# A conditioned attention, SwiGLU and ternary-MLP kernel: the order of the first batch's start on each engine, and finer waits there

## What is computed

```python
gamma, beta = t @ attn_gamma_w.T, t @ attn_beta_w.T        # per batch, 256 each
h = gamma * rmsnorm(x) + beta
q, k, v = h @ W_q.T, h @ W_k.T, h @ W_v.T                   # 16 heads of 16
x = x + alpha * (softmax(scale * q k^T) v) @ W_o.T
x = x + f_alpha * swiglu(f_gamma * rmsnorm(x) + f_beta)     # 1024 hidden
h = x * (1 + cond @ norm_w.T) * rsqrt(mean(x*x) + eps)
val, gate = split(h @ up_w.T)                               # 2 x 1024
y = act_quant(val * gelu(gate)) @ weight_quant(down_w).T + x
```

## Time and profile before

| what | value |
|---|---|
| median of 3 runs | 1111.65 us |
| lowest and highest run | 1110.89 and 1113.03 us |
| the profiled execution, own time | 1110.89 us |
| its span in the profile | 1109.1 us |
| its mean granted TensorE clock | 0.98 |
| busy: PE, DVE, ACT, POOL | 1037.1, 774.6, 562.6, 347.4 us |

### The profile page before, as it was taken

How to read it: one execution, slowest core, us unless ns; L and a number is a source line. 1 busy time by engine, 2 the same in 40 slices (tenths; PEclk the granted TensorE clock), 3 DMA queues, 4 the chain that set the end, 5 groups by cost and what they waited for, 6 DMA issues and landing times.

```text
span 1109.1 us, 19198 instructions
## 1 busy us (share of the span) xinstructions
PE 1037.1 (94%) x6775; PEld 719.0 (65%) x6775; DVE 774.6 (70%) x1556; ACT 562.6 (51%) x1260; POOL 347.4 (31%) x415
## 2 busy tenths in 40 slices
PE   6789889999999999999999999988989999899997
PEld 5333247755774775577567567744878878788775
DVE  4766686677578757866876696677647787466775
ACT  4355666557556655755665575556552333132221
POOL 2501123323242332424133332201332444243331
PEclk9889999999999999999999999998999999999998
DMA  8554433064234406332531623060311210002111
GB/s 252 150 92 154 76 104 132 15 110 125 87 45 111 148 21 111 101 111 30 121 116 58 111 71 123 12 139 20 97 53 29 59 57 30 29 29 63 58 53 38
DMA packets 89375, 92.71 MB, mean 84 GB/s; under 512 B 11856, under 2 KB 86616, under 8 KB 88256
## 3 DMA queue, kind: packets, MB, share of 16 engines
q1 hardware_dynamic: 87248, 89.59, 31.1%
q10 hardware_dynamic: 2032, 1.90, 0.6%
HBM read 61.68 MB, written 29.78 MB: 82 GB/s over the span
## 4 chain that ended last, share of the span: by engine, by line
PE 77%; DVE 14%; issue 5%; DMA 2%; POOL 1%; ACT 1%; ACTq 0%; POOLq 0%; DVEq 0%
PE gen L1162 30%; PE core L1162 13%; PE pvb L1277 11%; PE core L1251 9%; PE core L1265 8%; DVE negmax L924 7%; PE gen L1488 2%; PE pvb L1480 1%; PE gen L1236 1%; DVE o L948 1%; PE pvb L1285 1%; PE gen L1315 1%; PE core L1255 1%; DVE qs L1112 1%; DMA shift_d<-shift 0%
## 5 line engine op out<-in xcount | busy, mean ns | idle before, releaser
L924 DVE TENSOR_REDUCE negmax<-core 128x1 f32<-128x512 f32 x512 | 337.5, 684 | 169.9 <-PE core L1251 169.0
L712 ACT ACTIVATE p<-core 128x512 f32<-128x512 f32 x512 | 278.5, 597 | 146.1 <-PE core L1265 143.5
L1162 PE MATMUL gen<-hs,wgh 128*128 128x256 f32 x1536 | 220.5, 294 | 9.7 <-DVE a L978 9.7
L1251 PE MATMUL core<-kst,qst 96*128 96x512 bf16 x512 | 193.7, 395 | 33.5 <-DVE negmax L924 27.7
L1162 PEld LDWEIGHTS gen<-hs,wgh 128*128 128x128 f32 x1536 | 196.2, 189 | 28.3 <-DVE a L978 14.8
L1162 PE MATMUL core<-wup,hp 128*128 128x512 f32 x768 | 190.7, 397 | 0.9 <-POOL hp L652 0.9
L603 POOL TENSOR_TENSOR a<-a 128x256 fp32r<-128x256 f32 x128 | 94.7, 740 | 290.3 <-ACT a L730 287.7
L1162 PEld LDWEIGHTS core<-wup,hp 128*128 128x128 f32 x768 | 140.2, 189 | 29.2 <-issue 0.9
L1265 PE MATMUL core<-qst,kst 99*128 99x512 bf16 x512 | 157.2, 387 | 0.1
L1251 PEld LDWEIGHTS core<-kst,qst 96*128 96x128 bf16 x512 | 46.0, 97 | 152.3 <-DVE negmax L924 77.4
L1277 PE MATMUL pvb<-p,vst 128*32 128x512 f32 x1024 | 127.7, 618 | 0.0
(11 more groups left out here) (158 smaller groups left out, 1234.0 us busy)
## 6 DMA issues: line engine op xcount, KB each, us to landing
parts_d<-qk SPq DMA_DIRECT2D x30, 384.0 KB, 2.7
v_d<-v SPq DMA_DIRECT2D x8, 1024.0 KB, 3.9
vst<-v_d SPq DMA_DIRECT2D x16, 512.0 KB, 5.4
qst<-parts_d SPq DMA_DIRECT2D x96, 64.0 KB, 2.3
qst<-parts_d SPq DMA_DIRECT2D x48, 128.0 KB, 4.5
kst<-parts_d SPq DMA_DIRECT2D x48, 128.0 KB, 7.7
kst<-parts_d SPq DMA_DIRECT2D x91, 64.0 KB, 2.3
xr<-in_x_dram SPq DMA_DIRECT2D x8, 512.0 KB, 4.0
```

The source lines that it names most:

```text
L712: act.activation(p32[:, ring(b, m), k * S:(k + 1) * S], stb[k], ACT.Exp, scale=SCALE).then_inc(s["exp_"], 1)
L924: dve.tensor_reduce(negmax[:, n // TT, n % TT:n % TT + 1], smb[n % 2], AX_X, ALU.max, negate=True).then_inc(s["smax"], 1)
L1162: last = pe.matmul(out_, l, r, start=start and i == 0, stop=stop and i == len(passes) - 1, **kw)
L1251: pe.matmul(smb[n % 2], qst[0:KROWS, h, q * P:(q + 1) * P], kst[0:KROWS, h, :], start=True, stop=True).then_inc(s["smax_mm"], 1)
```

## The change

Five edits, all of them in the start of batch 0:

1. DVE normalises x and splits weight group 0 before it waits for the tables' matmuls; the copies to `table` and `cur` follow (now `first_tables`).
2. The load of W_v has a semaphore of its own. Weight group 0 waits for W_q and W_k alone; groups 1 and 2 wait for W_v too.
3. The first projection waits for the low parts of two weight groups, the second for those of three.
4. The low part of K's first half is made by DVE behind `qk_rest(0, 1)` in place of POOL. It has a semaphore of its own (`first_kl`), for which SP, POOL and ACT wait where they waited for `qk_l`.
5. ACT issues the store of K's high part behind the middle part of Q and not ahead of it.

```diff
-                sp.wait_ge(s["qk_l"], 2)
+                sp.wait_ge(s["first_kl"], 1)
                 first_part(sp, 1, 2, "parts1_st")
...
-                pool.tensor_tensor(qk3[:, j % 2, 2, :], rest[j], qk3[:, j % 2, 1, :], ALU.subtract).then_inc(s["qk_l"], 1)
+                if (b, j) == (0, 2):
+                    pool.wait_ge(s["first_kl"], 1)
+                if (b, j) != (0, 1):
+                    pool.tensor_tensor(qk3[:, j % 2, 2, :], rest[j], qk3[:, j % 2, 1, :], ALU.subtract).then_inc(s["qk_l"], 2 if (b, j) == (0, 2) else 1)
...
-                act.dma_start(raw_qkv[...], w[n]...).then_inc(s["raw_qkv_load"], 16)
+                act.dma_start(raw_qkv[...], w[n]...).then_inc(s["raw_v_load" if n == "W_v" else "raw_qk_load"], 16)
...
                 act.copy(qk3[:, j % 2, 0, :], gen[QK_BANK[j]][:, :]).then_inc(s["qk_h"], 1)
-                if (b, j) == (0, 1):
-                    act.wait_ge(s["qk_h"], 2)
-                    first_part(act, 1, 0, "first_kh")
...
-                    act.wait_ge(s["qk_l"], j - 1)
+                    act.wait_ge(s[("qk_l", "first_kl")[j % 2]], 1)
                 act.copy(qk3[:, j % 2, 1, :], rest[j]).then_inc(s["qk_m"], 1)
+                if (b, j) == (0, 0):
+                    act.wait_ge(s["qk_h"], 2)
+                    first_part(act, 1, 0, "first_kh")
...
-            dve.wait_ge(s["tab_mm"], 1)
             nt, nf = NSC * KD, NFIRST * KD
-            dve.tensor_copy(table[:, 0:nf, :]..., gen[1][:, 0:nf * B]).then_inc(s["tab_copy"], 1)
+            def first_tables():
+                dve.wait_ge(s["tab_mm"], 1)
+                dve.tensor_copy(table[:, 0:nf, :]..., gen[1][:, 0:nf * B]).then_inc(s["tab_copy"], 1)
+                dve.wait_ge(s["tab_copy"], 1)
+                dve.tensor_copy(cur[:, 0, 0:nf].unsqueeze(2), table[:, 0:nf, bass.ds(0, 1)]).then_inc(s["cur_set"], 1)
...
                 dve.tensor_tensor(rest[j], gen[QK_BANK[j]][:, :], qk3[:, j % 2, 0, :], ALU.subtract).then_inc(s["qk_r"], 1)
+                if (b, j) == (0, 1):
+                    dve.wait_ge(s["qk_m"], 2)
+                    dve.tensor_tensor(qk3[:, 1, 2, :], rest[1], qk3[:, 1, 1, :], ALU.subtract).then_inc(s["first_kl"], 1)
...
                         if b == 0:
-                            dve.wait_ge(s["tab_copy"], 1)
-                            dve.tensor_copy(cur[:, 0, 0:nf].unsqueeze(2), table[:, 0:nf, bass.ds(b, 1)]).then_inc(s["cur_set"], 1)
+                            xnorm(b, 1, xa, TT)
+                            split_lo(WG_QKV, "qkv_hi", "qkv_lo", qkv_bank, 0, 1)
+                            first_tables()
                         ...
-                        if b == 0:
-                            xnorm(b, 1, xa, TT)
-                            split_lo(WG_QKV, "qkv_hi", "qkv_lo", qkv_bank, 0, 1)
...
-            pe.wait_ge(s["raw_qkv_load"], 16 * 3)
+            pe.wait_ge(s["raw_qk_load"], 16 * 2)
             transpose_weights(WG_QKV, "qkv_t", "qkv_lo", qkv_bank, 0, 1)
...
-                    if b == 0:
-                        pe.wait_ge(s["qkv_lo"], len(WG_QKV))
+                if b == 0 and j < 2:
+                    pe.wait_ge(s["qkv_lo"], 2 + j)
...
                         if b == 0:
+                            pe.wait_ge(s["raw_v_load"], 16)
                             transpose_weights(WG_QKV, "qkv_t", "qkv_lo", qkv_bank, 1, 3)
```

More of the change, by code:

```diff
@@ L232, in build @@
         qkv_bank = [smb[1], stb[0], stb[1]]
-        names = """past raw_gate_load raw_hidden_load raw_out_load raw_up0_load raw_up1_load raw_down_load raw_qkv_load raw_o_load cond_load cond2_load ob_load ident_set consts_set cond_t cond_tc cw_t cw_tc cw2_t cw2_tc
-        tab_mm tab_copy tab2_mm tab2_copy stack_first first_qh first_qm first_kh first_km qkv_t qkv_hi qkv_lo row_mm row_copy row_ob alpha_stored kones
+        names = """past raw_gate_load raw_hidden_load raw_out_load raw_up0_load raw_up1_load raw_down_load raw_qk_load raw_v_load raw_o_load cond_load cond2_load ob_load ident_set consts_set cond_t cond_tc cw_t cw_tc cw2_t cw2_tc
+        tab_mm tab_copy tab2_mm tab2_copy stack_first first_qh first_qm first_kh first_km first_kl qkv_t qkv_hi qkv_lo row_mm row_copy row_ob alpha_stored kones
         wt_t wt_hi wt_lo cur_set cur2_set
@@ L684, in _ @@
             for i, n in enumerate(("W_q", "W_k", "W_v")):
-                act.dma_start(raw_qkv[:, KD * i:KD * i + KD, :], w[n].rearrange("(r p) i -> p r i", p=P)).then_inc(s["raw_qkv_load"], 16)
+                act.dma_start(raw_qkv[:, KD * i:KD * i + KD, :], w[n].rearrange("(r p) i -> p r i", p=P)).then_inc(s["raw_v_load" if n == "W_v" else "raw_qk_load"], 16)
             def other_tables():
@@ L874, in _ @@
             dve.tensor_copy(a32_flat[0:C, 0:NFIRST * D], core_flat[0:C, 0:NFIRST * D]).then_inc(s["cw_tc"], 1)
-            dve.wait_ge(s["tab_mm"], 1)
             nt, nf = NSC * KD, NFIRST * KD
-            dve.tensor_copy(table[:, 0:nf, :].rearrange("p n b -> p (n b)"), gen[1][:, 0:nf * B]).then_inc(s["tab_copy"], 1)
+            def first_tables():
+                dve.wait_ge(s["tab_mm"], 1)
+                dve.tensor_copy(table[:, 0:nf, :].rearrange("p n b -> p (n b)"), gen[1][:, 0:nf * B]).then_inc(s["tab_copy"], 1)
+                dve.wait_ge(s["tab_copy"], 1)
+                dve.tensor_copy(cur[:, 0, 0:nf].unsqueeze(2), table[:, 0:nf, bass.ds(0, 1)]).then_inc(s["cur_set"], 1)
             def other_tables():
```

## The result

| what | before | changed |
|---|---|---|
| median of 8 runs | 1109.92 us (1106.98 to 1113.03) | 1106.09 us (1104.93 to 1108.73) |
| the profiled execution, span | 1109.1 us | 1103.5 us |
| its mean granted clock | 0.98 | 0.983 |

The ratio is 0.9957 (95% interval 0.9938 to 0.9977): faster, by 2.6 to 6.9 us. I had forecast 1109.1, in 1107.3 to 1111.6. Two things have to be told apart: what the start gives, and what the rest of the kernel did. Two executions in the slow state, of 1313 and 3565 us (one of edit_5_alone and one of no_finer_waits), are left out of all means further down.

The account below looks back on a forecast made before the run. PE carries 77% of the chain, so the start of the first score was taken to decide. 1.95 us up to the first projection plus 0.65 behind it made 2.6, from 1111.65 to 1109.05 us; range 1107.3 to 1111.6.

Parts of the forecast that it names:

- Sum: Whole kernel: 1.95 us up to the first projection plus 0.65 behind it, 2.6 off the 1111.65 median, giving 1109.05.
- How the numbers follow: Chances and range for the whole kernel: forecast 0.50, faster 0.53 together, same 0.39, slower 0.08; about 1 us noise per case.
- a rival in which the change adds some: Later stages: more weighted matmul groups at half clock, each costing 1.5 us, up to 1115.2 us; chance 0.08.
- Steps 1 and 2: Start: x normalised ahead of the tables, W_v's load apart; x's transposes start 1.5 us plus 0.2 earlier, 1.8 with overlap.
- Step 3: First projection: finer waits give 0.15 us alone; with the earlier x it starts near 16.1, 1.9 to 1.95 us earlier.
- The two were level: Ahead of the first projection before: PE's queue ended at 17.90, DVE's low part of group 2 at 17.92.
- PE's queue takes over as the limit: First projection: finer waits give nothing beyond 0.15 us, since PE's own queue then sets the start.
- the clock rises early: Start: PE's clock rises at 14, DVE's group 1 sets the projection, 2.3 us up to there, 1108.7 in all; chance 0.12.
- Step 4: Between projections and first score: K's low part on DVE and ACT's new order give 0.65 us (0.1 to 0.85).
- DVE beside POOL: K's low-part subtraction on DVE while POOL does Q's: taken as 1.1 us, between 0.69 and 1.63.
- V: Projection ahead of the first score in PE's list: possible next limit, ending about 0.15 us earlier, at 30.2.

Follow-up runs that it names:

- edit_5_alone: Kernel before with only ACT's store of K's high part moved behind Q's middle part: mean 0.0 us against before, -0.3 at equal clock.
- no_finer_waits: Changed kernel with the first projection waiting for the low parts of all three weight groups: mean -1.5 us against the kernel before, -1.7 at equal clock.
- the repeated change: Changed kernel run once more beside the kernel before, 35 runs: medians 1107.04 against 1111.03 us, ratio 0.9969, -3.2 us at equal clock.
- edits_4_5: Kernel before with only K's low part on DVE and ACT's later store: mean +0.1 us against before, 0.0 at equal clock.
- stores_first: Changed kernel with SP's stores of both low parts ahead of Q's row loads: mean -2.6 us against the kernel before, -2.9 at equal clock.
- late_xa: Changed kernel with the load of batch 1's x issued behind the first stack: mean -4.2 us against the kernel before, -3.0 at equal clock.
- edit_4_alone: Kernel before with only K's low part moved to DVE, ACT's store unmoved: mean -0.3 us against before, -0.5 at equal clock.

## Why the prediction was right or wrong

**The mechanism was right.** x ahead of the tables, DVE idle there, PE's transposes brought forward, the new copies to `table` free, the queue of SP behind K's low part: these are in the rows as the prediction put them. The first score was forecast between 28.2 and 28.9, at 28.45 by the sum, and came at 28.36 and, in the second profile, 29.10. That 28.36 is so near to 28.45 is luck: the way to the projection gave 0.6 us more than forecast and the step behind it 0.5 less, and the landing of the store scatters by more than either. The gain was forecast at 2.6 us and measured at 3.2 (error 0.4) at equal clock.

**Where it failed: the starting point and the noise.** The working failed at "Sum", where the 2.6 us were taken from a median of 1111.65, and at "How the numbers follow", where each case was given "about 1 us of noise" from three runs that spread by 2.1. The kernel before has a standard deviation of 2.7 to 3.7 us within a session for single runs; the median of its first eight was 1109.92. Of the 3.0 us between the forecast of 1109.1 and 1106.09, 1.7 are that median, 0.6 are a gain larger than forecast, and 0.6 is what is left of the plain difference of 3.8; a mean clock 0.001 above the repeated change's is worth that and more (0.001 for 0.9 us), and this is luck. The range of 4.3 us was too narrow for a median of eight runs measured apart. The profile had shown the reason: eight stretches at half clock between 44 and 950 us, of which one that meets a weighted group is worth 1.5 us. I made them a rival in which the change adds some, and not the noise that every case carries in both directions.

**Steps 1 and 2** were sized at 1.8 us for the start of x's transposes and measured 1.98: L908 began at 8.16 and the tables' matmuls at 8.37, 0.34 earlier than in the kernel before, where I had given 0.2. PE overlaps the weight groups with the transposes ahead of them.

**Step 3** was sized at 0.15 for the finer waits and 1.95 for the sum with steps 1 and 2, with PE's queue as the limit. Measured: 2.57 in sum, and 0.6 for the finer waits. "The two were level" was true of that execution, and of edits_4_5, but not of the kernel. In edit_5_alone, which has the same start as the kernel before, the clock rose about two microseconds earlier, PE's queue was done and PE idled, and the projection still started at 18.05: DVE's low part of the last weight group was the limit. The statement "PE's queue takes over as the limit" depends on the clock in the same way. In the changed kernel's profile it rose near 14.5, which was the rival "the clock rises early" (2.3 for these steps, 0.12), and PE's queue and DVE were level. In stores_first it rose by 13.6, and PE idled until DVE's low part of group 1 was there, for the same start of the projection:

```profile
18.05 3.04 PE L1162 MATMUL gen<-hp,wqkv 128*128 128x512 f32 x12 [1.18 <-DVE wqkv L895]
```

```profile
15.50 3.04 PE L1171 MATMUL gen<-hp,wqkv 128*128 128x512 f32 x12 [0.47 <-DVE wqkv L903]
```

The first line is of edit_5_alone, the second of stores_first. Only in late_xa, where a group still took 1.06 at 14.46, did PE's queue set a later start, 16.03, which is the forecast's 16.1. The changed kernel itself, profiled twice, had a group of 1.06 us at 13.61 in one execution and of 0.60 at 13.43 in the other, with starts 0.1 apart. By the Trainium skill, "TensorE: Matmul & The Clock Gate", Part 1, the window runs free of a kernel's start; these two executions agree with that.

**Step 4** was sized at 0.65 and gave 0.18 in the changed kernel's profile. I had counted SP's queue from the end of Q's middle part, and left out the store of Q's high part, for whose landing SP's first row load waits. Moved 2.6 us earlier it falls among the loads and lands in 2.61 us. In edits_4_5, where that doesn't arise, 0.5 was gained up to the issue. And the landing of the next store scatters by more than the step is worth.

**DVE beside POOL** was put at 1.1 us (0.69 to 1.63) and took 0.90 here and 1.25 in edit_4_alone. The queue on SP hid both. The prediction says that no row shows this cost and takes L969 as the nearest. The trace of the kernel before had the pair itself: L1055 on DVE beside L574 on POOL, 1.09 us. It also had the neighbours of L969, as told in the last section.

**V** ended at 27.6 in the changed kernel, 0.8 ahead of the first score, and never became the limit.

## What to carry to other kernels

Take the noise of a kernel from its mechanism and not from three runs: where the granted clock falls in short stretches, regress runs on their clock before comparing them, and give the range that scatter. When work is brought forward, ask of each transfer in it what else is in flight at its new time. A finer wait that is worth nothing while two limits are level can be worth its full size once something else moves one of them.

## What the runs showed of the hardware that I had not expected

**DVE waits for POOL to end.** The subtraction of two SBUF tiles on DVE beside one on POOL. From the changed kernel's timeline, POOL ran from 19.74 to 20.90 and DVE from 20.55 to 21.45. From edit_4_alone:

```profile
22.98 1.17 POOL L583 TENSOR_TENSOR qk<-th,qk 128x512 bf16<-128x512 f32 x1 [6.67 <-ACT qk L756]
```

```profile
23.45 1.25 DVE L959 TENSOR_TENSOR qk<-ug,qk 128x512 bf16<-128x512 f32 x1 [0.86 <-ACT qk L756]
```

DVE ended at 24.70, POOL at 24.15. In both, DVE ends 0.55 us behind POOL, though it started 0.35 ahead of POOL's end in the one and 0.70 in the other. The 1.09 us of `h`'s low part in both kernels fit the same count: POOL ended at 14.18 in the changed kernel, DVE at 14.74. Without POOL beside it an instruction of this kind, L969 at 743.60, took 0.69; so about 0.14 of it passes before it is held and 0.55 follows when POOL is done.

The same count explains the spread of L969, which the prediction left open. One of its eight, in the kernel before:

```profile
148.81 2.96 POOL L574 TENSOR_TENSOR hp<-h,hp 128x512 fp32r<-128x512 f32 x2 [24.14 <-ACT hp L705]
```

```profile
149.28 1.36 DVE L969 TENSOR_TENSOR x<-th,xr 128x512 f32<-128x512 f32 x1
```

POOL's first ran 1.28 us, until 150.09; DVE ended at 150.64, 0.55 behind it. POOL's second began at 150.05, while DVE still worked, and took 1.72: it is held by DVE in its turn. The six L969 of 1.35 to 1.63 us all stand beside such a pair and end 0.54 to 0.55 behind POOL's first. Of the two of 0.69, one had no POOL instruction beside it (743.60), and the other began 0.15 ahead of POOL's large one (853.74). A DVE subtraction with one input in PSUM is not held: L903 at 26.42 in the changed kernel took 0.69, all of it while POOL worked on its own (26.11 to 27.29). So while POOL works on two SBUF tiles, a DVE instruction with two SBUF inputs hardly moves, and the overlap of such a pair gains almost nothing.

**Half clock costs most of what PE loses by it.** 0.001 of the mean clock is 2.2 us at half clock in a span of 1109 us, in which PE loses 1.1 us of work. The fits give 0.82 to 0.96 us for it, as if PE were the limit for most of those stretches; that isn't shown stretch by stretch.

**A store's landing scatters.** The store of 128 KB that stands last in the burst took 3.7, 3.8, 3.9, 3.9, 4.0, 4.2, 4.4, 4.6, 4.6, 4.7, 4.8 and 5.3 us in twelve profiles (all but the two in which it doesn't stand last), against 1.7 for the first stores of the same size where nothing else is in flight, as in the kernel before at 20.33. What sets the landing isn't shown.
